# Queries and keys of the second attention as fp32r products of split tokens and weights, a bank per token tile

## The reference

```python
x = x + _L1_attn_ref(_layernorm(x, axis=-1), L1_attn_wq, L1_attn_wk, L1_attn_wv, L1_attn_wo)
# in _L1_attn_ref
q = jnp.einsum('bsd,hkd->bhsk', x, wq.reshape(H, dk, D))
k = jnp.einsum('bsd,hkd->bhsk', x, wk.reshape(H, dk, D))
v = jnp.einsum('bsd,hkd->bhsk', x, wv.reshape(H, dk, D))
q = _apply_rope(q, sin, cos)
k = _apply_rope(k, sin, cos)
```

## Time and profile before

| | |
|---|---|
| median of 3 runs | 896.26 us (895.15 to 899.03) |
| the profiled execution | 897.05 us |
| its span, first to last instruction | 895.0 us |
| mean granted TensorE clock | 0.994 of full speed |
| TensorE, DVE, ACT, POOL busy | 97%, 69%, 48%, 11% of the span |

### The profile page before, as it was taken

How to read it: one execution, slowest core, us unless ns; L and a number is a source line. 1 busy time by engine, 2 the same in 40 slices (tenths; PEclk the granted TensorE clock), 3 DMA queues, 4 the chain that set the end, 5 groups by cost and what they waited for, 6 DMA issues and landing times.

```text
span 895.0 us, 13929 instructions
## 1 busy us (share of the span) xinstructions
PE 869.9 (97%) x5281; PEld 669.3 (75%) x5281; DVE 619.2 (69%) x1154; ACT 430.5 (48%) x1079; POOL 98.1 (11%) x79
## 2 busy tenths in 40 slices
PE   8998999999999999999989999999979999999998
PEld 5665778888888876767767777767657788888886
DVE  4669756666665756667778888889757666666665
ACT  7554543434343468883344444445365443344342
POOL 4001000000000150000321323223200000000000
PEclk9999999999999999999999999999999999999999
DMA  7003111111100410013100000000201111111001
GB/s 192 1 2 126 36 53 49 40 53 53 35 0 1 178 76 1 2 71 129 68 1 1 1 2 1 1 1 1 89 18 37 53 37 53 53 49 39 18 1 47
DMA packets 12535, 37.33 MB, mean 42 GB/s; under 512 B 2080, under 2 KB 4352, under 8 KB 11712
## 3 DMA queue, kind: packets, MB, share of 16 engines
q1 hardware_dynamic: 12448, 36.58, 12.6%
q0 software_dynamic: 32, 0.01, 0.0%
HBM read 35.54 MB, written 1.05 MB: 41 GB/s over the span
## 4 chain that ended last, share of the span: by engine, by line
PE 84%; DVE 8%; ACT 5%; issue 2%; POOL 1%; DVEq 0%; ACTq 0%; POOLq 0%
PE ps L1437 78%; PE ps L2083 3%; PE ps L1610 2%; DVE probs_q L931 1%; DVE P L586 1%; ACT Q L1200 1%; ACT probs_q L1332 1%; POOL outer_rot L1430 1%; DVE rope_buf L865 1%; DVE xn L518 1%; ACT DT L1017 1%; DVE stats L510 1%; DVE wlo L852 0%; DVE neg_max L921 0%; ACT h_hi L1245 0%
## 5 line engine op out<-in xcount | busy, mean ns | idle before, releaser
L1245 ACT ACTIVATE h_hi<-weighted_h 128x512 fp32r<-128x512 f32 x100 | 63.2, 632 | 150.3 <-DVE weighted_h L736 148.1
L746 DVE TENSOR_TENSOR h_lo<-weighted_h,h_hi 128x512 fp32r<-128x512 f32 x100 | 69.2, 692 | 66.1 <-ACT h_hi L1245 65.9
L1437 PE MATMUL ps<-xT_second,whi 128*128 128x512 f32 x376 | 108.5, 391 | 0.2 <-ACT silu_g L1240 0.2
L1437 PE MATMUL ps<-xT_first,whi 128*128 128x512 f32 x376 | 108.6, 390 | 0.0
L773 DVE TENSOR_TENSOR shared_gate<-silu_g,row_shares 128x512 f32<-128x512 f32 x88 | 60.9, 692 | 61.9 <-ACT silu_g L1240 61.6
L1240 ACT ACTIVATE silu_g<-ps 128x512 f32<-128x512 f32 x100 | 59.7, 598 | 73.4 <-PE ps L1437 73.4
L1437 PEld LDWEIGHTS ps<-xT_second,whi 128*128 128x128 f32 x376 | 70.1, 188 | 15.6 <-issue 1.1
L1437 PEld LDWEIGHTS ps<-xT_first,whi 128*128 128x128 f32 x376 | 70.3, 188 | 15.1 <-issue 0.5
L1332 ACT ACTIVATE probs_q<-ps,neg_max 128x256 f32<-128x256 f32 x128 | 58.7, 485 | 45.9 <-DVE neg_max L921 45.9
L1437 PE MATMUL ps<-h_hi,wlo 128*128 128x512 f32 x200 | 78.0, 390 | 0.0
L1437 PE MATMUL ps<-h_hi,whi 128*128 128x512 f32 x188 | 74.2, 395 | 0.4 <-DVE h_lo L746 0.3
(11 more groups left out here) (212 smaller groups left out, 1652.4 us busy)
## 6 DMA issues: line engine op xcount, KB each, us to landing
raw<-in_ffn SPq DMA_DIRECT2D x50, 384.0 KB, 3.0
wx<-in_wx SPq DMA_DIRECT2D x4, 2112.0 KB, 8.1
cx<-in_cx SPq DMA_DIRECT2D x1, 1536.0 KB, 6.4
X<-in_x SPq DMA_DIRECT2D x4, 256.0 KB, 7.1
kvc<-in_kvc SPq DMA_DIRECT2D x1, 1024.0 KB, 14.3
out<-X SPq DMA_DIRECT2D x4, 256.0 KB, 2.2
wqkv<-in_wqkv SPq DMA_DIRECT2D x1, 768.0 KB, 8.5
wqkv<-in_wqkv SPq DMA_DIRECT2D x1, 512.0 KB, 6.2
```

The costliest lines, as they stand in the source:

```text
L746: v.tensor_tensor(h_lo[:, u % 2, :], weighted_h[:, u % 2, :], h_hi[:, u % 2, :].bitcast(F32), ALU.subtract).then_inc(act_lo[l], 1)
L1245: a.activation(h_hi[:, u % 2, :], weighted_h[:, u % 2, :], ACT.Copy).then_inc(act_hi[l], 1)
L1437: return pe.matmul(o, l, r, start=start, stop=stop, skip_group_check=True)
```

## The change

Both operands of the query and key products are split into fp32r parts. The weights are split once into `wqk`, inside `experts(0)` at half chunk n = 9: the high part by ACT, the rest by DVE. The tokens of each batch are split out of bank 7 into `split_tokens` (two batches in turn): the high part by ACT ahead of the `xT4` copy, the rest by DVE (`tokens_rest1`), which needs bank 7 to stay as it is. So the turn of the next batch into bank 7 now waits for DVE too. TensorE then does, for each token tile `st` of 128 tokens, six products of 512 columns (256 of queries and 256 of keys) into one bank. The rotation takes a bank of that new layout, and POOL starts on a batch when both of its banks are rotated. Values stay fp32. The other changes to semaphores are renamings and shifted counts.

```diff
             # SBUF
+                split_tokens = sb("split_tokens", [P, 2, 2, KD, SEQ], F32R, c=projections)
+                wqk = sb("wqk", [P, 2, KD, 2 * D], F32R, c=layer1)
             # DVE
+            def tokens_rest1(b):
+                v.wait_ge(xt_ready, NB + b + 1)
+                v.tensor_tensor(split_tokens[:, 1, b % 2], ps[:, 7, :].rearrange("p (k s) -> p k s", k=KD), split_tokens[:, 0, b % 2].bitcast(F32), ALU.subtract).then_inc(xt_rest, 1)
             def attention1():
                 for b in range(NB - 1):
-                    for j in range(2):
-                        project1(b, j)
+                    if b >= 1:
+                        tokens_rest1(b + 1)
+                    for st in range(2):
+                        project1(b, st)
...
+                        if l == 0 and isinstance(n, int) and n == 9:
+                            v.wait_ge(wqk_split, 1)
+                            v.tensor_tensor(wqk[:, 1, :, :].rearrange("p k (j d) -> p k j d", j=2), wqkv1[:, 0:2, :, :].rearrange("p j k d -> p k j d"),
+                                            wqk[:, 0, :, :].bitcast(F32).rearrange("p k (j d) -> p k j d", j=2), ALU.subtract).then_inc(wqk_split, 1)
...
                 add_experts(l, 1)
                 if l == 0:
+                    tokens_rest1(0)
                     normalise(3, 2)
+                    tokens_rest1(1)
                     normalise(3, 3)
             # ACT
             def transposed_tokens(i, b):
                 a.wait_ge(pe_xt, i + 1)
+                if i >= NB:
+                    a.activation(split_tokens[:, 0, b % 2], ps[:, 7, :].rearrange("p (k s) -> p k s", k=KD), ACT.Copy)
                 a.activation(xT4[:, :, b, :], ps[:, 7 if i >= NB else PIECE_BANK["x"], :].rearrange("p (k s) -> p k s", k=KD), ACT.Copy).then_inc(xt_ready, 1)
...
+                        if l == 0 and isinstance(n, int) and n == 9:
+                            a.wait_ge(w1_loaded, 16)
+                            a.activation(wqk[:, 0, :, :].rearrange("p k (j d) -> p k j d", j=2), wqkv1[:, 0:2, :, :].rearrange("p j k d -> p k j d"), ACT.Copy).then_inc(wqk_split, 1)
             # POOL
-                    g.wait_ge(rope_done, 6 * b + 3 * j + 3)
+                    g.wait_ge(rope_done, 6 * b + 6)
             # TensorE, transposed_tokens
                 if b >= 1:
                     pe.wait_ge(xt_ready, i)
+                if l == 1 and b >= 1:
+                    pe.wait_ge(xt_rest, b)
             # TensorE, attention1
-                def query_or_key(b, j):
+                pe.wait_ge(wqk_split, 2)
+                def queries_and_keys(b, st):
+                    pe.wait_ge(xt_rest, b + 1)
                     if b >= 2:
-                        pe.wait_ge(rope_done, 6 * (b - 2) + 3 * j + 3)
-                    tokens(1, rope_bank(b, j), j, b).then_inc(pe_f, 1)
+                        pe.wait_ge(rope_done, 6 * (b - 2) + 3 * st + 3)
+                    for m, (x, w) in enumerate(((0, 0), (0, 1), (1, 0))):
+                        for kk in range(KD):
+                            last = mm(ps[:, rope_bank(b, st), :], split_tokens[:, x, b % 2, kk, 128 * st:128 * st + 128], wqk[:, w, kk, :], m + kk == 0, m + kk == 3)
+                    last.then_inc(pe_f, 1)
```

## The result

The changed kernel takes 901.96 us (median of 6 runs, 900.49 to 902.97) against 896.31 us for the kernel before in the same comparison (6 runs, 894.85 to 899.3). The ratio is 1.0053, with a 95% interval of 1.0032 to 1.0074: slower, by 2.9 to 6.6 us. Two later comparisons gave 1.0073 (1.0052 to 1.0095) and 1.0076 (1.0051 to 1.0100). The forecast was 899.1 us with a range up to 901.8; the median lies 0.2 us above that end, and the ratio applied to the 896.26 us that the forecast started from gives 901.0, inside it. By the line of 0.5% (900.7 us) that the prediction drew between the same and slower, this is just slower, to which it had given a chance of 0.21. The profiled execution after took 900.49 us with a span of 898.7, against 897.05 and 895.0 before.

What follows compares the result with a forecast made beforehand. The prediction took TensorE, busy 97% of the span, as the bound. Its terms, 3.85 - 2.7 + 1.7 = +2.9 us on the median of 896.26 us, gave 899.1 us, with a range of 896.3 to 901.8 us.

Steps and rivals of the forecast that it cites:

- Term 1: Query and key products on TensorE: fp32r at 0.227 us each in place of fp32, 2.7 us less over four batches.
- Term 2: TensorE's turn of batch 1 waits at bank 7 for DVE's subtraction behind four additions: 3.85 us more.
- Term 3: The new wait brings one fall to half clock over the stage's first products: 1.7 us more, bounds 0 and 3.4.
- A: The forecast itself: hold at bank 7 and one fall of the clock, 899.1 us; chance 0.68.
- B: The hold at bank 7 comes but the clock stays up, 897.4 us; chance 0.13.
- C: Half clock lasts two stretches, over batch 0's turn and values behind the wait, 901.0 us; chance 0.11.
- From step 2 on of the scores: Everything from there to the kernel's end shifts by the same amount, the chain running unbroken through TensorE and ACT.
- rival E: The new query and key products cost what the fp32 ones cost: +5.6 us, 901.8 us; chance 0.04.
- (a): Weight split in the experts costs nothing, hidden by 0.15 us before TensorE's load; 0 to 0.3 us in the range.
- (b) to (d): No cost: batch 1's subtraction has 2.4 us of slack, DVE keeps up for batches 2 and 3, POOL has 1.3 us.
- (e): No DMA is moved; SP's loads after the experts hang on DVE's additions, which stay: no cost.
- D: TensorE doesn't wait, its turn of batch 1 finding bank 7 free; only the saving is left, 893.6 us; chance 0.04.

Runs made afterwards that it cites:

- e7: e4 with queries and keys as the fp32 products of the kernel before, split tokens and weights unread; 898.59 us, ratio 1.0023 to the kernel before.
- e4: Changed kernel with DVE's subtraction for batch 0 ahead of the experts' second-half additions; 894.46 us, ratio 0.9975 to the kernel before; again 896.38 us, 0.9998.
- e1: Kernel before plus only a wait of TensorE's turn of batch 1 for a normalised tile on DVE; 900.7 us, ratio 1.0050 to the kernel before.
- e2: Changed kernel with 15 unread fp32r products ahead of TensorE's wait for bank 7; 896.97 us, ratio 1.0002 to the kernel before.
- e5: e4 with TensorE doing batch 0's values before turning batch 1, and one normalisation moved later; 898.05 us, ratio 0.9990 to the kernel before.
- after_again: Changed kernel, unedited, profiled again; stage 32.01 us, +1.29 us against the kernel before, with no half clock at the hold.
- before_look2: Kernel before, unedited, profiled a second time; single time 895.33 us.

## Why the prediction was right, and where it was not

**Term 1, the products (2.7 us less): right in sum, its parts off.** The distance is 0.234 us, not the 0.227 of the earlier trace rows; batches 0 to 2 save 1.9 us, not 2.18. Batch 3, for which I had taken 0.5 of 0.73 us, gave 0.64 (the shift fell from 4.50 us at the first scores to 3.87 at ACT's first copy). Sum 2.6, shown by e7 against e4.

**Term 2, the hold (3.85 us): right.** TensorE goes on at 303.96 us in an execution that is 0.07 us ahead, 3.85 us late. It was found from DVE's order and four rows, by asking what stands ahead of the new releaser.

**Term 3, the clock (1.7 us, one fall): right in kind and in the mean at the hold, wrong as a fixed number.** In the stage the four profiles show 2.65, 0, 1.5 and 2.7 us beyond the +1.28 of terms 1 and 2, on average 1.7. Rivals A, B and C all happened, in different executions of one kernel. The stage of the changed kernel is +3.0 us on average, where the sum said +2.9. The Trainium skill's page "TensorE: Matmul & The Clock Gate", section "HAM oscillation — how this bites in real kernels", puts the price of a fall at half of the throttled time. By the table the rest grows by half a microsecond for each at 0.5, so the traces agree on the price. That a wait of this length brings a fall held in three profiles of four.

**The step that failed: "From step 2 on of the scores, everything down to the end is shifted by the same amount".** The sum stopped at the stage. Measured is +4.8 us by the ratio and 5.65 by the medians, and 1.9 to 2.8 us of it are missing in the sum. The profiles have them behind the stage, most of them in the waits of the cross attention, 300 us later: 12.5 us at half clock on average against 6.6 before, 3.0 us of work, which with the stage's 3.0 makes 6.0. Term 3 put the whole cost of the clock at 1.7 us, and by the runs it is 4.1. I had taken the falls there for a fixed cost of both kernels; I had also left out a fourth fall of the kernel before, which begins 1.1 us before its end and costs next to nothing.

Why the changed kernel has more of them isn't settled. The hold is not a sufficient cause (e1's profile has it and 4.5 us in the rest, and its runs 13.0 in all; e2's runs have 8.8) nor a necessary one (e5 lacks it and has 15.8 and 14.0). Chance in the choice of profiles doesn't explain it either: the runs have 18.5 against 10.2 us, and none of the 15 runs of the changed kernel is below 900.1 us.

**What was luck.** The upper end of the range, 901.8 us, came from rival E, products as dear as the fp32 ones. That did not happen, and without E the range would have ended at C's 901.0, where the ratio puts the result. The sum itself is 1.9 to 2.8 us short of the measurement, so that the number came out inside or at the edge of the range for another reason than the one that set it.

**The covers.** (a) The weight split is hidden, as worked out: ACT's copy 133.17 to 134.21, DVE's 134.24 to 135.47, the `h_lo` of n = 10 from 137.49 to 138.18, and TensorE loads for it at 138.44:

```profile
133.17 1.04 ACT L1297 ACTIVATE wqk<-wqkv 128x1024 fp32r<-128x1024 f32 x1
...
134.24 1.23 DVE L801 TENSOR_TENSOR wqk<-wqkv,wqk 128x1024 fp32r<-128x1024 f32 x1 [0.25 <-ACT wqk L1297]
...
137.49 0.69 DVE L757 TENSOR_TENSOR h_lo<-weighted_h,h_hi 128x512 fp32r<-128x512 f32 x1 [0.70 <-ACT h_hi L1264]
...
138.44 0.19 PEld L1459 LDWEIGHTS ps<-h_hi,whi 128*128 128x128 f32 x1
```

The margin is 0.26 us, against 0.15 forecast. (b) to (d): from 299 to 330 us TensorE has one wait over 0.1 us, the one at bank 7, and none for POOL; by after_again's +1.29 us nothing else is lost. (e) No experiment tests it, and no wait in the stage points to a DMA.

**Rivals D and E** didn't happen: TensorE waits 3.7 us for DVE in all four profiles, and the products are cheaper than fp32 (e7).

## What to carry to other kernels

Ask of every new wait what stands ahead of its releaser on the releaser's engine: here a saving of 2.6 us was bought with a wait of 3.85, and moving one subtraction ahead of four additions took 2.9 us of it back. A wait on TensorE also put the clock at risk: here it cost its length and zero to 2.7 us more at the wait itself, and over the whole kernel 4.1 us more went to the clock than before. So take the mean from several profiles, and the time at half clock from the mean granted clock of every run. A sum of one stage is a forecast of the stage; where the rest of the kernel hangs on chance events, cut the profiles at the stage's end and compare the parts.

## What was not expected of the hardware

The same wait of 3.7 us gave 0, 3.4 or 6.8 us at 1.2 GHz in four executions of one kernel. In the cross attention the length went with the time from TensorE's stop to the fall, in all 14 profiles. Waits of 2 us elsewhere gave falls in some executions and none in others (460 us: a fall in before, none in before_look2).

Fifteen products without a reader, laid into a wait, are worth about 5 us in the median of a kernel of 900.

fp32r products of 512 columns follow each other at 0.227 us in the experts and at 0.234 here, at the same clock; the cause stays open.
